# Self attention's q, k and v from pairs of half-precision numbers, and the first cross-attention queries loaded in another order

## The reference

```python
# layer 0
x = x + self_attention(ln(x), w_qkv, w_proj)      # causal, 16 heads of 16
x = x + cross_attention(ln(x), ctx, mask, Wq, Wk, Wv, Wo)   # ctx: (2, 77, 192)
x = x + experts(ln(x), Wg, bg, We, be)            # 8 linear experts, top 2
# layer 1
x = x + rnn(ln(x), Wi, bi, Wh, bh)                # h = tanh(xt + h @ Wh.T + bh), 1024 steps
x = x + cross_attention(ln(x), ctx, wq, bq, wk, bk, wv, bv, wo, bo)
x = x + gated_experts(ln(x), ...)                 # 16 routed experts, top 4, and a shared one
```

```python
qkv = x @ w_qkv.T
q, k, v = jnp.split(qkv, 3, axis=-1)
scores = jnp.einsum('blhd,bmhd->bhlm', q, k) * scale   # then causal mask, softmax, @ v, @ w_proj.T
```

## Time and profile before

| | us |
|---|---|
| median of three runs (1419.01 to 1427.31) | 1423.26 |
| the profiled execution, its whole time | 1424.58 |
| its span in the trace | 1422.8 |
| PE busy | 1374.9 (97%) |
| PE weight loads busy | 938.5 (66%) |
| DVE busy | 845.1 (59%) |
| ACT busy | 626.7 (44%) |

### The profile page before, as it was taken

One profiled execution on the slowest core, in us unless ns is written; L12 is line 12 of the kernel. 1 busy time (PEld: TensorE's weight loads), 2 busy tenths in 40 slices (PEclk: granted clock), 3 DMA queues, 4 the chain that ended last, 5 costly groups with the idle time before them and its releaser, 6 DMA issues.

```text
span 1422.8 us, 48634 instructions
## 1 busy us (share of the span) xinstructions
PE 1374.9 (97%) x19892; PEld 938.5 (66%) x19892; DVE 845.1 (59%) x2658; ACT 626.7 (44%) x2838; POOL 37.9 (3%) x60
## 2 busy tenths in 40 slices
PE   6699889999999999999999999999999999999998
PEld 4466346777756777776677778775667677766554
DVE  5746774268775226978761226767555665448585
ACT  2062314843524784252258874561443335432422
POOL 2000000000000000000000001000000000000000
PEclk9899889999999999999999999999999899989999
DMA  5654100021000002120000002310000200002000
GB/s 152 101 139 95 57 1 2 3 50 16 3 2 3 3 3 40 33 33 3 2 4 3 3 3 99 92 26 2 2 2 18 39 3 3 17 2 38 2 16 16
DMA packets 45472, 40.22 MB, mean 28 GB/s; under 512 B 9723, under 2 KB 44486, under 8 KB 45254
## 3 DMA queue, kind: packets, MB, share of 16 engines
q1 hardware_dynamic: 43526, 36.32, 11.3%
q10 hardware_dynamic: 1728, 0.79, 0.5%
HBM read 25.81 MB, written 10.80 MB: 26 GB/s over the span
## 4 chain that ended last, share of the span: by engine, by line
PE 92%; DVE 4%; DMA 1%; ACT 1%; issue 1%; SPq 0%; DVEq 0%; ACTq 0%
PE b L515 23%; PE b L1613 9%; PE b L534 8%; PE b L1390 6%; PE b L1003 6%; PE b L974 5%; PE b L740 5%; PE b L1681 5%; PE b L919 4%; PE b L696 3%; DVE mx L928 3%; PE b L1259 3%; PE b L1234 2%; PE b L651 2%; PE b L459 2%; PE b L501 1%
## 5 line engine op out<-in xcount | busy, mean ns | idle before, releaser
L515 PEld LDWEIGHTS b<-hp,whp 128*128 128x128 f16 x12276 | 472.2, 96 | 258.3 <-ACT hp L560 170.8
L515 PE MATMUL b<-hp,whp 128*128 128x2 f16 x12276 | 533.0, 165 | 1.3 <-ACT hp L560 0.3
L566 DVE TENSOR_TENSOR hp<-hist,hp 128x4 f16<-128x4 f32 x1023 | 165.3, 162 | 412.7 <-ACT hist L561 402.1
L560 ACT ACTIVATE hp<-b 128x4 f16<-128x4 f32 x1024 | 177.5, 173 | 446.1 <-PE b L515 433.6
L928 DVE TENSOR_REDUCE mx<-b 128x1 f32<-128x512 f32 (+3 forms) x304 | 188.2, 653 | 0.5 <-PE b L922 0.5
L988 ACT ACTIVATE vp<-b 128x512 f32<-128x512 f32 x288 | 171.3, 603 | 19.7 <-PE b L977 11.8
L561 ACT ACTIVATE hist<-b 128x4 f32<-128x4 f32 x1024 | 178.4, 174 | 0.0
L534 PE MATMUL b<-whp 128*128 128x512 f16 (+6 forms) x624 | 168.8, 347 | 0.0
L1613 PE MATMUL b<-vp,heads 128*128 128x512 f16 x576 | 161.0, 384 | 0.0
L919 PE MATMUL b<-heads 128*128 128x512 f16 (+3 forms) x384 | 113.3, 334 | 4.7 <-DVE mx L928 1.6
L1390 PE MATMUL b<-we,xT 128*128 128x512 f16 x384 | 106.6, 385 | 0.0
(11 more groups left out here) (217 smaller groups left out, 1637.9 us busy)
## 6 DMA issues: line engine op xcount, KB each, us to landing
x_qs<-qx_scr SPq DMA_DIRECT2D x48, 128.0 KB
qx_scr<-xq_pair SPq DMA_DIRECT2D x16, 256.0 KB, 2.1
heads<-q_scr SPq DMA_DIRECT2D x24, 128.0 KB, 4.2
heads<-k_scr SPq DMA_DIRECT2D x36, 64.0 KB, 2.6
x<-in_x SPq DMA_DIRECT2D x8, 256.0 KB, 6.5
q_scr<-tail SPq DMA_DIRECT2D x8, 256.0 KB, 2.4
k_scr<-tail SPq DMA_DIRECT2D x8, 256.0 KB, 2.3
x_qs<-in_L_ffn_We SPq DMA_DIRECT2D x2, 1024.0 KB, 7.3
```

Of the source, the lines that this page charges most:

```text
L515: return pe.matmul(self.z(t)[:, m], self.w.whp[:, a, k, m * P:(m + 1) * P], self.g.hp16[:, (t - 1) % 2, part, k, :], start=False, stop=Tru ...
L560: act.activation(self.g.hp16[:, t % 2, 0], self.z(t), ACT.Tanh, scale=1 / LIFT).then_inc(self.s["hi_ready"], 1)
```

## The change

It does five things.

1. The q, k, v weights are lifted by 64 and split into a high and a low half-precision part (`qkv_high` on ACT, `qkv_low` on DVE, four pieces each), and so is each normalised tile (`store1` on ACT gives the high part, the new `store1_low` on DVE the low one). A block of q or k is then six half-precision products of 512 columns (high by high, low by high, high by low), v of a tile six of 256 columns; the results are scaled by 1/64 where they are read.
2. The split weights lie in `x_pr`, which cross attention's first `exp` overwrites; so that waits (`guard_cross`) until all q, k, v are made. The recurrence's weights are loaded into `xT2` in place of `x_pr`.
3. Both `load_q` issue the rows of zeros first, before they wait for the queries.
4. For the first and the last chunk of cross attention, half of the query loads are issued by ACT (`load_q2`).
5. `load_second` 1, `rows_k` and `load_k` of layer 1 are placed behind cross attention's first `load_q`. Some semaphores are merged.

```diff
+        self.per = 3 * KD if self.paired else B * KD
+        st.add("pe", name + "_make", self.make_pairs if self.paired else self.make, N * M * per,
+               0.216 if self.paired else 0.43, lambda i: rank(i // (M * per)) + 0.09,
...
+    def make_pairs(self, pe, i):
+        n, part, k = i // self.per, i % self.per // KD, i % KD
...
+        if part == 0 and k == 0:
+            o = self.st.take(pe, self.name, n)
+            pe.wait_ge(*w.w_in)
+            pe.wait_ge(norm.s["stored"], TC * (c + 1))
+        wt, x = ((0, 0), (1, 0), (0, 1))[part]
+        last = pe.matmul(o[:], self.block(n // self.M, n % self.M)[0][:, wt, k], self.xT[:, x, k, :],
+                         start=part == 0 and k == 0, stop=part == 2 and k == KD - 1)
...
-        last = pe.matmul(o[:, 0:D], self.xT[:, k, column(j):column(j) + P], self.w.wqkv[:, k, 2 * D:3 * D],
-                         start=k == 0, stop=k == KD - 1)
+        acc(pe, o[:, 0:D], [(self.xT[:, x, k, column(j):column(j) + P], self.w.wqkv[:, wt, k, 2 * D:3 * D])
+                            for wt, x in ((0, 0), (1, 0), (0, 1)) for k in range(KD)]).then_inc(self.s["vmade"], 1)
...
-        st.add("sp", name + "_rows_k", self.rows_k, 2, 5.2, early, after=4.0, behind=later)
+        st.add("sp", name + "_rows_k", self.rows_k, 2, 5.2, early, after=4.0,
+               behind=later + [(name + "_load_q", lambda layer: layer)])
...
-        st.add("sp", name + "_load_q", self.load_q, N, 5.0, lambda n: rank(n) + 0.21, after=8.0)
+        self.shared = [0, N - 1]
+        st.add("sp", name + "_load_q", self.load_q, N, lambda n: 3.0 if n in self.shared else 5.0,
+               lambda n: rank(n) + 0.21, after=7.0)
+        st.add("act", name + "_load_q2", self.load_q2, 2, 2.0, lambda i: rank(self.shared[i]) + 0.21, after=7.0)
...
-            act.activation(xT1[:, :, column(i):column(i) + P], ln1.bank(i), ACT.Copy).then_inc(ln1.s["stored"], 1)
+            act.activation(xT1[:, 0, :, column(i):column(i) + P], ln1.bank(i), ACT.Copy).then_inc(s["n1_high"], 1)
+
+        def store1_low(v, i):
+            v.wait_ge(s["n1_high"], i + 1)
+            at = column(i)
+            v.tensor_tensor(xT1[:, 1, :, at:at + P], ln1.bank(i), xT1[:, 0, :, at:at + P], ALU.subtract
+                            ).then_inc(ln1.s["stored"], 1)
...
         def guard_cross(act):
 
             act.wait_ge(s["prepared"], 3)
+            over(act)
...
         st.add("sp", "load_second", load_second, 3, 2.5, lambda i: (-3400, 190, 990)[i], after=5.0,
-               behind=[("self_load_k0", lambda i: 1)])
+               behind=[("self_load_k0", lambda i: 1), ("x_load_q", lambda i: min(i, 1))])
...
+        st.add("act", "qkv_high", qkv_high, 2 * KD, 0.5, lambda i: -10)
+        st.add("v", "qkv_low", qkv_low, 2 * KD, 0.5, lambda i: -10)
```

More of the change, by code:

```diff
@@ L743, in make @@
             last.then_inc(self.s["made"], 1)
+    def make_pairs(self, pe, i):
+        n, part, k = i // self.per, i % self.per // KD, i % KD
+        c, w, norm = self.chunks[n // self.M]
+        o = self.st.bank(self.name, n)
+        if part == 0 and k == 0:
[5 more added lines that the diff above has]
+                         start=part == 0 and k == 0, stop=part == 2 and k == KD - 1)
+        if part == 2 and k == KD - 1:
+            last.then_inc(self.s["made"], 1)
     def part1(self, act, n):
@@ L750, in part1 @@
         out, src = self.pair[:, n % 2, 0], self.st.bank(self.name, n)[:]
-        if bias is None:
+        if self.paired:
+            act.activation(out, src, ACT.Copy, scale=1 / LIFT).then_inc(self.s["part1"], 1)
+        elif bias is None:
             act.activation(out, src, ACT.Copy).then_inc(self.s["part1"], 1)
@@ L878, in load_q @@
             sp.wait_ge(self.s["s2"], self.chunk_scores[c - 1])
+        for p in range(2):
+            row = 64 * p + ROWS
+            sp.dma_start(self.qs[row:row + 1, :, :], self.w.zero_row.unsqueeze(1).broadcast_to([1, H, CW])
+                         ).then_inc(self.s["q_in"], 16)
+        self.proj.wait_kept(sp, c, (0, 1))
         for p in range(2):
@@ L1124, in rows_k @@
             sp.wait_ge(sem, count)
-        rows = self.s[f"k_rows{layer}"]
+        rows = self.s[f"k_in{layer}"]
         for p in range(2):
@@ L1180, in load_q, with load_heads, load_q2 @@
                          ).then_inc(self.s["q_in"], 16)
+        self.proj.wait_kept(sp, n, (0, 1))
+        for p in range(1 if n in self.shared else 2):
+            self.load_heads(sp, n, p)
+    def load_heads(self, engine, n, p):
+        for r, (part, _) in enumerate(PARTS):
+            row = 64 * p + DH * r
+            engine.dma_start(self.qs[row:row + DH, :, :],
+                             self.q_scr[part, :, CW * n:CW * n + CW].rearrange("(r p d) t -> p d r t", p=2, d=DH)[p]
+                             ).then_inc(self.s["q_in"], 16)
+    def load_q2(self, act, i):
+        n = self.shared[i]
+        self.proj.wait_kept(act, n, (0, 1))
+        act.wait_ge(self.s["oned"], 2)
+        if n:
+            act.wait_ge(self.s["s2"], 2 * B * NG * n)
+        self.load_heads(act, n, 1)
     def first_pass(self, pe, i):
```

100 lines of the change are left out of this document (54 added, 46 removed).

## The result

The changed kernel takes 1410.91 us in the median of 20 runs (1403.07 to 1420.88), the kernel before 1423.84 in 20 runs beside it (1414.37 to 1434.59). The ratio is 0.9932 with a 95% interval of 0.9912 to 0.9953: faster by 0.7%. The forecast was 1412. The profiled execution of the changed kernel has a span of 1408.3 us, against 1422.8.

The account below looks back on a forecast made before the run. PE work was taken to bound recurrence and tail, PE, DVE and load handovers the start. First tanh −7.7, recurrence +2.7 and tail −6.4 gave −11.4 on the 1422.8 us span, so 1412 us; range 1402 to 1421.

Parts of the forecast that it names:

- the tail: After the last step: loses 7.1 us of PE work, gains 0.7 of filler, −6.4 us.
- rival A: Start: all 8.8 us of added DVE work stand on its path, start gains about nothing; 1420 us, chance 0.22.
- the ten maxima among the gates: Right before the experts: ten cross-attention maxima moved between the dependent gate operations, 10 × 0.6 = +6 us.
- gave the loads zero: Cross attention's query loads: moving them ahead and letting ACT issue some counted as zero; ACT's issues cost about 1.3 us.
- Steps 1 to 3: Start up to cross attention's memset: earlier scores −3.1, shorter projections −2.3 and −1.3; memset 6.7 us earlier, about 123.1.
- I cost them at nothing: Very beginning: weight splits and chunk 0's low parts (3.7 us of DVE) hidden in DVE's load waits; uncovered, up to 3.7.
- the 5.35 us wait at 51.18 goes: Chunk 1's first projection: its wait for ACT's store vanishes; chunk 0's maxima can begin about 2 us earlier.
- PE's relief: Start: half-precision projections take 10.2 us off PE, 6.9 in q and k, 3.3 in v.
- Step 4: Memset to first tanh: 17 maxima fewer before the first cross maximum, −8.5; +7.5 returned later; net −1.0 us.
- The recurrence: Recurrence steps: moved expert products and scores (4.5, 2.6, 0.9 us) less 5.3 of filler, net +2.7 us.
- rival B: Before the first tanh: 17 moved maxima fall into waits, costing 1 us rather than 7.5; 1405 us, chance 0.09.
- C (clock): Experts and cross attention: TensorE's clock stays low, +26 us against −11.4; 1438 us, chance 0.09.

Follow-up runs that it names:

- zeros_alone: The kernel before with only the rows of zeros issued ahead of the queries in both query loads; 1424.38 us, ratio 1.0031.
- numbers_behind: The kernel before with two planner numbers for cross attention's query load changed and layer 1's loads placed behind its first one; 1410.55 us, ratio 0.9945.
- loads_alone: The kernel before with only the load edits (zeros first, ACT issuing query loads, layer 1's loads behind) and full-precision projections; 1414.93 us, ratio 0.9931.
- short_make: The kernel before, order held, with each second q, k, v product of self attention cut from 256 to 128 columns; 1416.61 us, ratio 0.9970.
- numbers_alone: The kernel before with only the planner's two numbers for cross attention's query load changed (cost 3.0 for 5.0, after 7.0 for 8.0); 1418.43 us, ratio 0.9967.
- more_dve: The kernel before, order held, with 24 more DVE reductions ahead of self attention's normalised tiles, results unread; 1420.56 us, ratio 0.9982.
- pairs_alone: The changed kernel with all load edits taken back; 1419.80 us, ratio 0.9975 to the kernel before.
- numbers_best: The kernel before, full precision, with layer 1's loads behind cross attention's first query load and other planner numbers; 1402.72 us, ratio 0.9867.

## Why the prediction was right

**The sum was right, two of its causes were not, and it came out by luck.** In the profiles the five steps missed by +8.7 us (up to the memset), -1.5, -4.5, -6.4 and +0.6 (the tail), which add up to -3.1: an error in the start that would have ended in rival A's range was made good by three on the other side. The counts came from the order of both kernels, which holds whatever made it. So the terms that rest on counted instructions held in sign and roughly in size: the stretch from the memset to the first cross maximum (-8.5 forecast, -10.0 measured), the ten maxima among the gates (+6 forecast, 8.75 - 4.30 = +4.5 measured), the tail (-6.4 and -5.8). But I headed them as effects of the change as a whole and gave the loads zero. The loads' real order is worth zero (`zeros_alone`, and `numbers_behind` against `loads_alone`), and the planner's two numbers and the `behind` that came with them are worth all of the gain that the intervals can tell.

**Steps 1 to 3, the start up to the memset: wrong.** Forecast -6.7, measured +2.0, and +3.6 against `zeros_alone`, which has the order of before without the slow projections. Two sentences failed. "I cost them at nothing": DVE had idle time at the beginning, but the split stands ahead of the norms, and the first turn came 3.2 us later. And "the 5.35 us wait at 51.18 goes": it came down to 2.13 and moved to a later product. The size of PE's relief itself was right as far as `short_make` shows (5.8 to 7.3 us at the memset), though its parts were not: v brought 0.4 us in place of 3.3, q and k 12.5 in place of 6.9. I had priced what the engines do and not what each tile and each load then waits for. What was on the path is k leaving 2.0 us later, maxima that take 1.4 us longer, and PE's wait of 2.93 us at 116.50; how much of this is the low part and how much the new order stays open. By its own signs the prediction was wrong here: a low part is named as what PE waits for.

**Step 4, after the memset: right in sign, the return too large.** I gave +7.5 back behind the first cross maximum; it was +3.0. The gates took 1.5 us less than forecast, and the other maxima fell into waits: from the first cross maximum to the gates it took 42.99 us before and 41.71 after. That is rival B in part.

**The recurrence: the wrong term, its sign in part.** I summed +8.0 of moved products and -5.3 of filler to +2.7; measured -3.7. The filler of line 534 fell from 149.9 us to 142.3, 7.6 us, more than counted. Up to step 640 the difference is -3.56, and about the same in each kernel with these numbers (-3.6 in `numbers_alone`, -3.8 in `numbers_behind`). The same order as before takes 631.4 and 631.3 us up to there in `short_make` and `more_dve`, which lack a short fall of the clock that the kernel before has at 389 us, so the plan's own share is 2.1 to 3.6 us. From 640 on, the time goes with the falls of the clock: 423.6 us before, 423.4 after, 407.2 in `pairs_alone`, 431.1 in `loads_alone`, 415.8 in `numbers_best`, with few low windows in the short ones and many in the long ones. These are single executions, and with the order of before this part took from 416.9 (`more_dve`) to 423.8 us (`zeros_alone`). So two profiles can't tell what the change did to it; -3.7 for the whole recurrence lies within that spread. This term was in no part of my range.

**Rivals.** A (DVE carries it) holds in part of its result, the start's lost gain, and not in its cause. C (clock) did not come where I had put it: the experts' first 24 products took 6.83 us. The clock fell in the recurrence instead, where I had taken 0.98 as given. I had also misread a row for C: the granted clock in 129.80 to 152.00 was 0.92, and the 0.56 that I gave is the DMA share beside it, so C's case for a low clock there was weaker than written. And half of the experts' products at the lower level would be 8 us, not 11.4; taken alone, it would have needed over two thirds of them.

## What to carry to other kernels

Where a planner fixes the order, an edit has two effects, the work and the plan. Make a kernel that changes only the plan's numbers, and one that changes only the work with the order held, before giving either of them the credit. Then try other numbers alone: here they were worth more than the arithmetic.

A product that becomes cheaper on PE but needs one more engine ahead of it must be priced along the way of one tile, not by busy times. Adding DVE operations that nobody waits for cost at most 1.5 us of 6.7 at the memset; with the operations that PE does wait for, the cheaper products' gain did not arrive. That their way through three engines is the reason is argued here, not shown.

A wait that a profile names need not be new or on the path. Look for it in the trace of the kernel before, and ask whether the chain of waits goes through it: the 6.25 us for the low part stood there before under another name, and PE's next wait took them in.

When the times of one program spread by 1%, compare a stage between two profiles only where the clock was the same in both, or take another profile.

## What the hardware showed that I had not expected

The granted clock fell inside the recurrence while PE counted as busy for 19.89 of 20.00 us (0.66 in 920 to 940). The falls came back in the same windows in a second execution of the same program, but with the same instructions in the same order they partly sat elsewhere (1100 to 1120: 0.66 and 254 records of PE in the kernel before, 1.00 and 336 in `more_dve`). What sets them off is open. The section of the Trainium skill that the prediction named ("TensorE: Matmul & The Clock Gate", "Why this matters for your kernels") warns of idle gaps between bursts of products; here the windows show no gap of PE to blame, although a busy PE in these records includes small products of two columns.

The times of one program spread over 10 to 20 us from execution to execution, and this spread goes with the clock. Each of the changed kernel's 20 runs has its span and mean granted clock on record: they go from 1400.6 us at 0.985 to 1418.0 us at 0.970, with a correlation of -0.96; in the other kernels with 12 runs it is -0.69 to -0.99. The two profiled executions, which differ by 0.5 us in the recurrence and 0.1 in the span, had 0.977 and 0.979: they are two alike out of a wide spread. Why one execution has more falls than another is open too.
